# Up-projection on split high and low parts: five matrix products per tile in place of six

## The reference

```
xn2 = layernorm(x, ln2_g, ln2_b)
h = jax.nn.gelu(xn2 @ mlp_w1 + mlp_b1, approximate=False)     # 192 -> 768
return x + (h @ mlp_w2 + mlp_b2)                              # 768 -> 192
```

```
m = layernorm(h, g2, be2)
m = jax.nn.gelu(m @ fc1_w + fc1_b, approximate=False) @ fc2_w + fc2_b
return m + residual
```

## Time and profile before

| what | value |
|---|---|
| median of three runs | 1115.77 us (1110.28, 1115.77, 1119.21) |
| time of the profiled execution | 1113.01 us |
| its span | 1111.2 us |
| mean granted TensorE clock | 0.959 |
| busy: PE, DVE, ACT, POOL | 1033.5, 847.2, 700.6, 170.7 us |
| up-products (L1023, `ps<-xnt_all,w_up`) | 432, 75.0 us busy, 326 ns each |
| down-products (L1023, `ps<-w_dn,hid`) | 864, 77.5 us busy, 249 ns each |

### The profile page before, as it was taken

One profiled execution on the slowest core, in us unless ns is written; L12 is line 12 of the kernel. 1 busy time (PEld: TensorE's weight loads), 2 busy tenths in 40 slices (PEclk: granted clock), 3 DMA queues, 4 the chain that ended last, 5 costly groups with the idle time before them and its releaser, 6 DMA issues.

```text
span 1111.2 us, 35967 instructions
## 1 busy us (share of the span) xinstructions
PE 1033.5 (93%) x15606; PEld 731.5 (66%) x15606; DVE 847.2 (76%) x1714; ACT 700.6 (63%) x1003; POOL 170.7 (15%) x142
## 2 busy tenths in 40 slices
PE   5867889999999999999999999999989889998998
PEld 3545246665777776677776767676657776775776
DVE  4837978889999999999999999999526764233443
ACT  4646157677787777777777877777865442231554
POOL 4430000910000000000000000000024544001443
PEclk9885579999999999999999999999999999999999
DMA  4698967657474756565656566554400001211110
GB/s 122 172 223 271 239 119 167 107 99 129 85 121 93 111 97 107 96 107 101 103 100 105 104 99 108 96 95 88 80 13 21 25 23 34 68 54 41 40 45 23
DMA packets 83011, 109.17 MB, mean 98 GB/s; under 512 B 14109, under 2 KB 75234, under 8 KB 82661
## 3 DMA queue, kind: packets, MB, share of 16 engines
q1 hardware_dynamic: 82853, 106.87, 48.9%
HBM read 85.40 MB, written 21.44 MB: 96 GB/s over the span
## 4 chain that ended last, share of the span: by engine, by line
PE 71%; DVE 12%; DMA 7%; ACT 5%; issue 3%; POOL 2%; SPq 0%; DVEq 0%; ACTq 0%; POOLq 0%
PE ps L1028 35%; PE ps L1189 17%; PE ps L1023 15%; DVE mx_p L1485 4%; DVE xh L101 2%; POOL rstd L109 1%; DMA m_d<-mneg 1%; DVE stage_lo L1454 1%; PE ps L1041 1%; ACT hid_f L955 1%; DVE stats L88 1%; DMA rel_d<-stage_lo 1%; DMA rel<-in_c_rel_w 1%; PE ps L1135 1%; DMA qv<-m_d 1%
## 5 line engine op out<-in xcount | busy, mean ns | idle before, releaser
L1485 DVE TENSOR_REDUCE mx_p<-ps 128x1 f32<-128x464 f32 (+1 forms) x1080 | 608.6, 629 | 34.4 <-PE ps L1028 23.2
L905 ACT ACTIVATE prob<-ps 128x768 f32<-128x768 f32 x648 | 496.2, 810 | 184.9 <-PE ps L1028 184.1
L1028 PE MATMUL ps<-kc,qc 112*32 112x464 f16 (+1 forms) x4320 | 460.4, 370 | 8.6 <-issue 4.4
L1028 PE MATMUL ps<-qv,ka 113*32 113x384 f16 x5184 | 403.8, 328 | 10.3 <-DMA qv<-m_d 7.7
L1189 PE MATMUL ps<-prob,v_ext 128*32 128x384 f32 x2592 | 293.3, 487 | 2.5 <-issue 2.0
L1028 PEld LDWEIGHTS ps<-qv,ka 113*32 113x32 f16 x5184 | 213.9, 97 | 86.7 <-issue 28.6
L1028 PEld LDWEIGHTS ps<-kc,qc 112*32 112x32 f16 x4320 | 173.2, 95 | 108.0 <-DVE mx_p L1485 30.0
L1189 PEld LDWEIGHTS ps<-prob,v_ext 128*32 128x32 f32 x2592 | 117.0, 111 | 17.4 <-issue 3.2
L1023 PE MATMUL ps<-w_dn,hid 128*96 128x192 f16 x864 | 77.5, 249 | 6.6 <-DVE hid L1540 4.4
L1023 PEld LDWEIGHTS ps<-w_dn,hid 128*96 128x96 f16 x864 | 73.2, 125 | 12.0 <-issue 6.1
L752 POOL COPY v_ext<-v_all 128x288 f32<-128x288 f32 x12 | 5.1, 427 | 480.6 <-PE ps L1189 480.5
(11 more groups left out here) (106 smaller groups left out, 838.2 us busy)
## 6 DMA issues: line engine op xcount, KB each, us to landing
qv<-rel_d SPq DMA_DIRECT2D x216, 144.0 KB
qv<-kq_d SPq DMA_DIRECT2D x108, 216.0 KB
qc<-rel_d SPq DMA_DIRECT2D x24, 216.0 KB, 4.0
xin<-in_x SPq DMA_DIRECT2D x12, 288.0 KB, 3.3
kq_d<-khl SPq DMA_DIRECT2D x24, 144.0 KB, 2.3
q_h<-kq_d SPq DMA_DIRECT2D x9, 288.0 KB, 4.7
q_w<-qw_d SPq DMA_DIRECT2D x9, 288.0 KB, 6.7
rel_d<-stage_hi SPq DMA_DIRECT2D x4, 648.0 KB, 7.6
```

The source lines that it names most:

```text
L905: nc.scalar.activation(prob[:, s4(p, s), :].rearrange("p (a b) -> p a b", a=2), ps[:, 3 + 2 * (s % 2):5 + 2 * (s % 2), 0:CW], ACT.Exp).the ...
L1028: ins = nc.tensor.matmul(ps[c:c + 32, bank, 0:w], l[:, c:c + 32], r, start=True, stop=True, tile_position=(0, c))
L1485: nc.vector.tensor_reduce(mx_p[:, q * GT + k // MP, k % MP:k % MP + 1], ps[:, slot, 0:min(MW, N - k % MP * MW)], AX, ALU.max).then_inc(uni ...
```

## The change

The channels are split 128 and 64. The first 128 have their own high and low parts (`x[:, 0]` and `x[:, 1]`). The last 64 have theirs on top of each other in one operand, `x[:, 2]`: high on rows 0 to 63, low on rows 64 to 127. The high weights of these 64 channels are there twice, on rows 0 to 63 and on 64 to 127. A hidden tile then takes five products: high by high and low weight by high input over 128 rows, low weight by high input over 64 rows, high weight by low input over 128 rows, and one over 128 rows that gives high by high and high by low of the 64 channels at once. The norm's transposes become four of 128 columns and four of 64. The high copy on ScalarE and the low subtraction on VectorE become two instructions each. Gains and shifts of the two later norms are loaded in two transfers each, and the up weights in two transfers, the second of which reads its rows twice.

```diff
-        w_up = [sb("w_up0", [C2, 2, 2, HID], F16)]
+        w_up = [sb("w_up0", [128, 2, 2, HID], F16)]
-            xnt_all = sb("xnt_all", [C2, NC, 2, 2, CW], F16, r)
+            xnt_all = sb("xnt_all", [128, NC, 3, CW], F16, r)
...
-            load(eng, gain[1][:, :], d["L0_conv_ln2_g"].rearrange("(k p) -> p k", p=C2))
-            load(eng, shift[1][:, :], d["L0_conv_ln2_b"].rearrange("(k p) -> p k", p=C2))
-            load(eng, gain[2][:, :], d["L1_conv_g2"].rearrange("(k p) -> p k", p=C2))
-            load(eng, shift[2][:, :], d["L1_conv_be2"].rearrange("(k p) -> p k", p=C2))
+            for dst, nm in ((gain[1], "L0_conv_ln2_g"), (shift[1], "L0_conv_ln2_b"),
+                            (gain[2], "L1_conv_g2"), (shift[2], "L1_conv_be2")):
+                load(eng, dst[:, 0:1], d[nm][0:128].rearrange("(p o) -> p o", o=1))
+                load(eng, dst[0:C - 128, 1:2], d[nm][128:C].rearrange("(p o) -> p o", o=1))
...
                 sp.wait_ge(s_ps, step)
-                sp.dma_start(w_up_f[i][:, :, :], d[up].rearrange("(k p) n -> p k n", p=C2)).then_inc(w_mlp_in, 16)
+                sp.dma_start(w_up_f[i][:, 0, :], d[up][0:128, :]).then_inc(w_mlp_in, 16)
+                sp.wait_ge(s_ps, step + 1)
+                sp.dma_start(w_up_f[i][:, 1, :], d[up][128:C, :].unsqueeze(0).to_broadcast([2, C - 128, HID]))\
+                  .then_inc(w_mlp_in, 16)
                 sp.wait_ge(s_ps, step + 2)
...
-                for k in range(2):
-                    nc.scalar.activation(xnt_f[:, k, :], ps[0:C2, bank + k, 0:CW], ACT.Identity,
-                                         bias=shift[1 + i][:, k:k + 1], scale=gain[1 + i][:, k:k + 1])\
+                x = chunk_of(xnt_all, c)
+                for k, m in enumerate((128, C - 128)):
+                    nc.scalar.activation(xnt_f[0:m, k, :], ps[0:m, bank + k, 0:CW], ACT.Identity,
+                                         bias=shift[1 + i][0:m, k:k + 1], scale=gain[1 + i][0:m, k:k + 1])\
                       .then_inc(done, 1)
                 act.wait_ge(done, 2 * c + 2)
-                nc.scalar.activation(chunk_of(xnt_all, c)[:, :, 0, :], xnt_f[:, :, :], ACT.Copy).then_inc(x_hi, 1)
+                nc.scalar.activation(x[:, 0, :], xnt_f[:, 0, :], ACT.Copy)
+                nc.scalar.activation(x[0:C - 128, 2, :], xnt_f[0:C - 128, 1, :], ACT.Copy).then_inc(x_hi, 1)
...
-                transposes(xh2[0], bank).then_inc(done, 1)
+                for k, m in enumerate((128, C - 128)):
+                    for t in range(CT):
+                        ins = nc.tensor.transpose(ps[0:m, bank + k, t * T:(t + 1) * T],
+                                                  xh2[0][:, t, k * 128:k * 128 + m], ident[0:T, 0:T])
+                ins.then_inc(done, 1)
...
-                    for k in range(2):
-                        for part in range(2):
-                            mm(ps[:, m % 2, 0:CW], w_up[i][:, k, part, m * 128:(m + 1) * 128], x[:, k, 0, :],
-                               start=(k == 0 and part == 0), stop=False)
+                    w, o = w_up[i][:, :, :, m * 128:(m + 1) * 128], ps[:, m % 2, 0:CW]
+                    mm(o, w[:, 0, 0, :], x[:, 0, :], stop=False)
+                    mm(o, w[:, 0, 1, :], x[:, 0, :], start=False, stop=False)
+                    mm(o, w[0:C - 128, 1, 1, :], x[0:C - 128, 2, :], start=False, stop=False)
 
                 def lo_products(m):
-                    for k in range(2):
-                        ins = mm(ps[:, m % 2, 0:CW], w_up[i][:, k, 0, m * 128:(m + 1) * 128], x[:, k, 1, :],
-                                 start=False, stop=(k == 1))
+                    w, o = w_up[i][:, :, :, m * 128:(m + 1) * 128], ps[:, m % 2, 0:CW]
+                    mm(o, w[:, 0, 0, :], x[:, 1, :], start=False, stop=False)
+                    ins = mm(o, w[:, 1, 0, :], x[:, 2, :], start=False)
                     ins.then_inc(sems["up_ps"], 1)
...
-                nc.vector.tensor_tensor(x[:, :, 1, :], xnt_f[:, :, :], x[:, :, 0, :], ALU.subtract).then_inc(x_lo, 1)
+                nc.vector.tensor_tensor(x[:, 1, :], xnt_f[:, 0, :], x[:, 0, :], ALU.subtract)
+                nc.vector.tensor_tensor(x[C - 128:128, 2, :], xnt_f[0:C - 128, 1, :], x[0:C - 128, 2, :],
+                                        ALU.subtract).then_inc(x_lo, 1)
```

More of the change, by code:

```diff
@@ L138, in build @@
         w_proj = sb("w_proj", [C2 + 1, 2, C])
-        w_up = [sb("w_up0", [C2, 2, 2, HID], F16)]
+        w_up = [sb("w_up0", [128, 2, 2, HID], F16)]
         w_dn = [sb("w_dn0", [128, 2, HM, C], F16)]
         b_up = [sb(f"b_up{i}", [128, HM]) for i in range(2)]
-        gain = [sb(f"gain{i}", [C2, 2]) for i in range(3)]
-        shift = [sb(f"shift{i}", [C2, 2]) for i in range(3)]
+        gain = [sb(f"gain{i}", [128 if i else C2, 2]) for i in range(3)]
+        shift = [sb(f"shift{i}", [128 if i else C2, 2]) for i in range(3)]
         rows = sb("rows", [T, 4, C])
@@ L196, in build @@
             o_sb = sb("o_sb", [128, 2, CW], F32, r)
-            w_up_f = [sb(f"w_up_f{i}", [C2, 2, HID], F32, r) for i in range(2)]
+            w_up_f = [sb(f"w_up_f{i}", [128, 2, HID], F32, r) for i in range(2)]
             w_dn_f = [sb(f"w_dn_f{i}", [128, HM, C], F32, r) for i in range(2)]
@@ L210, in build @@
         u_sb = sb("u_sb", [4 * KF, CT, C])
-        w_up.append(sb("w_up1", [C2, 2, 2, HID], F16))
+        w_up.append(sb("w_up1", [128, 2, 2, HID], F16))
         w_dn.append(sb("w_dn1", [128, 2, HM, C], F16))
-        xnt_f = sb("xnt_f", [C2, 2, CW])
+        xnt_f = sb("xnt_f", [128, 2, CW])
         y_sb = sb("y_sb", [T, CT, C])
@@ L359, in wait_consts @@
             eng.wait_ge(consts, ALL_CONSTS)
-        ALL_CONSTS = 16 * (2 + 4 + 2 + 4 + 3 + 1 + 2 + 2 * NB)
+        ALL_CONSTS = 16 * (2 + 8 + 2 + 4 + 3 + 1 + 2 + 2 * NB)
         assert GU * 6 == 2 * GS * 5
@@ L385, in chunk_of @@
         def chunk_of(x, c):
-            return x[:, ds(c, 1), :, :, :].rearrange("p o k l t -> p (o k) l t")
+            return x[:, ds(c, 1), :, :].rearrange("p o k t -> p (o k) t")
         def is_at(n, head):
@@ L756, in _ @@
             copy_v(1, 1)
-            pool.wait_ge(w_mlp_in, 64)
+            pool.wait_ge(w_mlp_in, 96)
             for w in w_up_f + w_dn_f:
```

## The result

The changed kernel takes 1136.91 us (median of 4 runs, 1134.07 to 1139.95) against 1116.27 us for the kernel before, measured beside it: a ratio of 1.0188 (95% interval 1.0158 to 1.0218), so 20.6 us slower. The prediction said 1121.5, range 1112 to 1130. The profiled execution took 1139.49 us (span 1137.7, mean clock 0.946), 26.5 us more than that of before.

A forecast was written before the change was run, and what follows sets the result against it. Block 0 bound by a VectorE, GpSimd and ScalarE chain, block 1 by TensorE with ScalarE level. Terms 0.8 + 3.0 + 1.8 + 0.5 = +6.1 us on the profiled 1113.0, 1119.1; on the median's footing 1121.5, range 1112 to 1130.

The forecast's parts named there:

- Term (e): Up weights' load: more bytes (576 to 768 KB) and one more SP issue ahead of `qv`, +0.5 us (0 to 2).
- (d): Attention: four more gain and shift loads on SP's queue delay the maximum's transfer at about 248 us, +1.8 us.
- (a): Up-projection: one product in six goes, 11.7 us of TensorE's time; -3.6 us on the path if the others keep their spacing.
- (b): Up-projection: two changes to and from 64 rows a tile, 0.093 us each, outweigh the saved product; +0.8 us together with (a).
- Rival 1: Up-projection: the 64-row operand streams like any other, so the saving stands; +0.2 us in all, 1116.0; chance 0.20.
- (c): Norms in both blocks: transposes with two changes (0.19 us), ScalarE's copy and VectorE's subtraction split in two; +3.0 us.
- Rival 3: Block 0: TensorE idles more and is granted the lower clock in more chunks; +5 on top, 1126; chance 0.06.

The follow-up runs named there:

- e1: Changed kernel, but the second half of the up weights loaded by two plain 64-row transfers in place of one that repeats its rows: 1128.3 us.
- e1b: Same code as e1, run again on a different chip: 1124.6 us.
- e3: e1 with the third product over all 128 rows, so no 64-row operand among the up-products: 1124.1 us.
- e16: Kernel before, gains and shifts of the later norms in eight loads of 128 and 64 rows, as in the changed kernel: 1120.6 us.
- e4: Kernel before, gains and shifts of the later norms in eight loads of 96 rows each in place of four: 1119.3 us.
- e15: Kernel before, six products a tile kept, but the third over 64 rows in place of 96: 1122.0 us.
- e6: e1 with the feed-forward weights' and other late loads moved from heads 0, 1, 2 to heads 2, 3, 4: 1124.8 us.
- e9: Changed kernel, feed-forward weights' loads, the repeating one included, issued from GpSimd's queue in place of SP's: 1131.4 us.
- e14: Changed kernel with plain up-weight loads, third product over 64 rows, all loads of later stages on GpSimd's queue: 1120.3 us.
- e2: Kernel before, up weights in two transfers, the second written as 2 x 48 rows without repeated rows: 1114.5 us.
- e10: Kernel before with its feed-forward weights' loads on GpSimd's queue: 1117.1 us.
- e12: Kernel before with every load of the later stages on GpSimd's queue: 1116.0 us.
- e8: Kernel before, second half of the up weights loaded from 48 rows that one transfer writes twice: 1119.9 us.
- e13: Kernel before, second half of the up weights loaded from 6 rows repeated 16 times: 1114.6 us.

## Why the prediction was wrong

**Term (e) is the step that failed.** It priced the second load by bytes and by one more issue: "+0.5", from 0 to 2. The runs put 8.6 us on its form alone (e1; 12.3 by the median of e1b), and the traces 12 to 16 (15.7 less the 3.8 of e3 or the -0.6 of e1). The prediction looked at a size (576 to 768 KB) and at a queue, not at how the access pattern is dealt to the DMA engines. The leading 2 of the broadcast stood in the diff. Bytes and issue were the small part indeed: e1 carries them all, with SP's issues as quick as before.

**(d)** had the right place, less than half the size and not the mechanism: +1.8 forecast from SP's issues alone, 4.1 measured (e16). The wait at 248 was to go to about 4 us and went to 4.97, which looks like a hit; but e4, with the same number of issues, left it at 2.36, and what grew in e16 was the maximum's round trip, 5.0 to 9.0 us.

**(a), (b)** were right where the result hangs on them. 0.093 us a change forecast, 0.100 measured (e15); the operand of 64 rows behaves as the of 32 columns, and the Trainium skill's drain at a change of mode (TensorEngine Tiling, Key Properties) is borne out for rows. Forecast for tiles 2 to 5: 0.024 each; the GELUs show 0.04. Rival 1, the free product, is dead. One reading in (a) was wrong: ScalarE does not need 0.98 us a tile. In e3 its GELUs start 0.87 us apart, so before the change TensorE alone set the pace. The time forecast does not hang on it, since the gain of (a) never came.

**(c)** had the transposes' two changes wrong: 0.88 for 0.86 us, though half of their weights are 64 columns wide, which by the same page's When to Use Tiling counts as column tiling. No run here shows whether these fp32 transposes are tiled at all. ScalarE's split copies start at 1075.15 and end at 1076.09, 0.94 in place of 0.84; forecast 0.93. With (b) it makes 14.59 - 14.34 = 0.25 a chunk of block 1; forecast 0.34. Forecast for both blocks: 3.8. Measured, the clock's play included: block 0 6.3 (mean of e1, e1b, e6, e9, e14 and after) less 2.0 (mean of the eight traces of runs e2 to e16 with the code of before), and 1.6 in block 1, 5.9. The excess is all in block 0. Its fourth and fifth chunks, measured between the starts of `xnt_f` where the clock was at 1.00, take 19.63 us with 64 rows (after, e1, e9) against 19.48 with the code of before (e4, e10, e12): +0.15, half of the 0.31 forecast. The first three chunks and the last cost more.

**Rival 3, the clock,** had a chance of 0.06. In block 0 the changed kernel's trace has 8.5 us in the measure of the table against 1.7, and 11.1 against 2.9 in the stalls of heads 0 and 1, where the prediction had not looked for it. It is part of the price of the load, and part of the 2 us by which the blocks are dearer than forecast, but not all: among traces with the same 3.4 in the clock column block 0 costs 4.8 and 4.9 with 64 rows (e6, e9) against 1.6 to 2.1 (e4, e8, e13), and with 5.1 it costs 6.1 (e14) against 3.1 to 3.4 (e10, e12, e16). That is about 3 us at like clock, where (b) and (c) had some 2 for block 0.

**The sum.** 8.6 for the load's form, 4.1 for the small loads, 5.9 for the blocks: 18.6 of 20.6 us. The last two, 10.0 together, should be what e1 and e1b cost over the kernel before, and these are 12.1 and 8.0. With e1b beside e1 the first term is 8.6 to 11 by the ratios (1.0188 - 1.0089 = 1.0%), so what is left open lies within the spread of the runs.

## To carry to other kernels

Read the outermost dimension of a new transfer before its size: two 64-row loads of the same bytes, or 16 copies of a few rows, cost nothing, while one load of two copies held up the transfers that followed it, from whichever queue it was issued. Small loads issued ahead of a latency-bound transfer can lengthen its round trip by more than their issues take (4.0 us for four issues of 0.45 more), and here by their rows rather than by their number. Before a product is dropped from a stream, look for operands of 64 rows or fewer among the rest; two changes a tile (0.2 us) cost more than the product saved (0.16). And where another engine leads a stage, look at the granted clock when TensorE gets less to do there: here 3.2 us won in block 1 left 4.2, 0.3 and 1.1 us in the medians of three pairs, and the rest went in block 0 with more time at the lower clock, though that link is not shown.

## What the hardware showed beyond expectation

A queue can look like the culprit and be innocent: SP was held 8.9 us, and with SP freed (2.2 us) the attention stayed 14 us late. A stall of 6.4 us (at 191 us) costs more than itself, since TensorE comes back at clock 0.50 (190.9 to 194.3 us). Weights of 96x64 between those of 96x128 cost no change in fp32 transposes, while fp16 products over 64 rows between 96 or 128 cost 0.10 us each way.
